# Six copies of the key stack issued from ScalarE's queue instead of SyncE's, in a two-layer attention, mixture and routing kernel

## The chip, the cores and the metric

The kernel runs on one core of one Trainium2 chip. The metric is the device time of one execution in microseconds (us); lower is better. The engines are TensorE (PE: matmuls, and PEld for its weight loads), VectorE (DVE), ScalarE (ACT), GpSimd (POOL) and SyncE (SP). SP does no arithmetic here: it only issues transfers (DMAs). ACT and POOL can issue them too, from queues of their own.

## The reference, cut to what matters

The data are `x`, 8 batches of 256 tokens of width 256, and a context of the same shape. There are four blocks in a row, each added to `x`:

```
x = x + cross_attention, self_attention and gelu FFN   # L0_xattn: two attentions, 16 heads of width 16
x = x + top-2 mixture of 7 experts and a no-op         # L0_ffn
x = x + cross_attention over the same context          # L1_xattn
x = x + gelu FFN on the top half of the tokens         # L1_ffn
# one attention:
q = split_heads(x @ qw + qb); k = split_heads(ctx @ kw + kb); v = split_heads(ctx @ vw + vb)
probs = softmax(q k^T / 4 + mask); out = probs v @ ow + ob
```

## The kernel before, in words

An attention of one batch is an *item*; there are 24 of them, numbered `n`. Items 0 to 7 are the cross attention and 8 to 15 the self attention of the first block; they run as one pipeline in the first third of the kernel. Items 16 to 23 are the third block's attention and form a second pipeline after the experts. Each engine's program is one list, merged by `side_by_side` from small generators: each `yield t` states a planned time in abstract steps, and pieces are put in order of these times. So the order on an engine is fixed, and an instruction that waits for a semaphore holds up everything behind it on that engine. `start_of(n)` is 8 steps after that of the item before; `kv_start(n)` is the same but for item 16.

The arithmetic is fp32 in quality, with each operand split in a high and a low part. For the scores, a head's product over 16 rows is done as one product over 48 rows: the *query stack* `qst` and the *key stack* `kst` hold, for each head pair, three groups of 16 rows (high, high, low against high, low, high), and two more rows for the mask and the row maximum. The stacks are laid out by DMA: `q_parts` and `k_parts` (128 partitions, high and low, two halves `s`) are copied to 16 partitions at a time, six copies for each stack (2 values of `s` by 3 values of `c`), each 128 KB. A stack has three buffers in turn (`NSET`), but `q_parts` and `k_parts` have one each.

One item goes as follows.

- PE transposes the item's rows (L210), projects queries and keys (L186 to L188, `G[0]`). ACT writes the high part of each (`high`, L792) and DVE the low part (`split`, L1163, which raises `q_split` or `k_split`). ACT's `high` of item n first waits until all six copies of item n-1 have landed, since they read the same buffer.
- SP issues the copies (L379). Its list for one item is: two small rows of maxima of an earlier item (L417, which waits for `m_row`), six query copies, for items 0 to 10 two copies of mask rows into `kst` (L396), six key copies (which wait for `k_split`), and then loads from HBM that fall due (raw weights L365, context L372).
- PE waits for both stacks, then runs for each of 8 head pairs `p` the scores (L528, into `S_PS`), from which DVE takes the row maximum (L1207). Later it transposes the maxima (L538); ACT writes them out (`m_hi`, L810, raises `m_row`).
- PE then computes the transposed scores (L549, into `T_PS`) with the maximum's row as part of the product; ACT takes the exponential of each pair (L818). `T_PS` is one buffer: the scores of the next pair wait for the exp before. PE multiplies the probabilities with the values (L588), and ACT copies the result out (L831). Transposes (L562), normalisation, the output projection and LayerNorm follow.

Three items are in work at once: while the scores of item n run, the exps of item n-1 or n-2 and the projections of item n+1 run between them. ACT's list around one item n+1 is: `k_parts` high, `m_hi`, exp, exp, copy out, exp, `hT_hi` (L801), exp, copy out, exp, copy out, exp, `q_parts` high, exp, copy out, `aT_hi` (L824), exp.

Of the kernel before, what the change touches and what calls it, by code (L numbers as in the profile page):

```python
# [6 lines left out]
F32 = mybir.dt.float32  # L7
# [7 lines left out]
B, S, D, H = 8, 256, 256, 16  # L15
DH = D // H
# [3 lines left out]
HG = H // 2  # L20
# [7 lines left out]
MASK_ROW = 3 * DH  # L28
MAX_ROW = MASK_ROW + 2
SROWS = MASK_ROW + 2  # L30
NA = 2 * B
NSET = 3
# [48 lines left out]
def build(nc, x, ctxT, mask, wA, colA, rowA, fi, fo, fib, rw, rb, ein, eout, wC, colC, rowC, w1, w2, b1, out):  # L81
# [14 lines left out]
    with scope[0] as root:  # L96
# [67 lines left out]
        kst, qst = stacks[0::2], stacks[1::2]  # L164
# [62 lines left out]
        ITEMS = range(3 * B)  # L227
# [25 lines left out]
        def kv_start(n):  # L253

            return T_E0 + 5 * E_STEP if n == NA else start_of(n)
# [66 lines left out]
        with nc.Block() as block:  # L322

            @block.sync
            def _(sp):
# [47 lines left out]

                def stack(n, which):
                    j = n % NSET
                    dst = qst[j] if which == "q" else kst[j]
                    for s in range(2):
                        for c in range(3):
                            sp.dma_start(dst[64 * s + DH * c:64 * s + DH * (c + 1), :, :].bitcast(F32), PARTS[which][c][:, s, :].bitcast(F32)).then_inc(sm[f"stk_{which}{j}"], 16)  # L379

                def stack_k(n):
                    j = n % NSET
                    yield kv_start(n) - 6.7
                    if n >= NA + NSET or NSET <= n < NA:
                        sp.wait_ge(sm["st_ps"], HG * (n - NSET + 1))
                    elif n >= NA:
                        sp.wait_ge(sm["kst_one"], n - NA + 1)
                    elif n:
                        sp.wait_ge(sm["init_p"], 2 * n)
                    else:  # L390
                        sp.wait_ge(sm["init_d"], 1)
                    if n < B + NSET:
                        sp.wait_ge(sm["mask_out"], 48)
                        src = mask_dram[n] if n < B else mask_dram[B]
                        for s in range(2):
                            sp.dma_start(kst[j][64 * s + MASK_ROW:64 * s + MASK_ROW + 2, :, :].bitcast(F32), src).then_inc(sm[f"mask_ld{j}"], 16)  # L396
                    sp.wait_ge(sm["k_split"], n + 1)
                    stack(n, "k")

                def stack_q(n):  # L400
# [9 lines left out]
                    else:  # L410
                        sp.wait_ge(sm["init_d"], 1)
                    stack(n, "q")
                    yield t0 + 8.9
# [33 lines left out]
                def store(i):  # L447
# [4 lines left out]
                side_by_side(setup(), weights(), *(context(n) for n in ITEMS if layer(n) != SELF),  # L452
                             *(stack_k(n) for n in ITEMS), *(stack_q(n) for n in ITEMS),
                             *(expert_weights(e) for e in range(NE)), *(expert_tokens(e) for e in range(NE)), *(expert_store(e) for e in range(NE)),
# [311 lines left out]
            def _(act):  # L766
# [14 lines left out]
                def high(n, which, at):  # L781
# [11 lines left out]
                    last.then_inc(sm[f"{which}_hi_s"], 1)  # L793

                def queries(n):
                    t0 = start_of(n)
                    yield t0 - 12.95
                    act.wait_ge(sm["hT_ps"], n + 1)
                    if n:
                        act.wait_ge(sm["v_ps"], n)  # L800
                    act.activation(flat(hT_hi[:]), G[0], ACT.Copy).then_inc(sm["hT_hi_s"], 1)  # L801
                    yield from high(n, "q", t0 - 10.1)
# [88 lines left out]
                def mod(i):  # L891
# [14 lines left out]
                    for m in range(KF):  # L906
                        yield t0 + 1 + 0.4 * m
                        act.wait_ge(sm["mfc1_ps"], 2 * i + m // 4 + 1)
                        if i >= 2 and m == 0:
                            act.wait_ge(sm["mfc2_ps"], i - 1)  # L910
                        act.activation(mg[:, i % 2, m, :], T_PS[:, m * P:(m + 1) * P], ACT.Gelu_apprx_tanh, bias=b1c[:, m:m + 1]).then_inc(sm["mgelu"], 1)

                side_by_side(setup(), *(queries(n) for n in ITEMS), *(high(n, "k", kv_start(n) - 8.1) for n in ITEMS), *(attention(n) for n in ITEMS),
                             *(ffn(f) for f in range(B)), *(route(g) for g in range(len(GROUPS))), *(expert(e) for e in range(NE)),
# [527 lines left out]
```

## Time and profile before

| | |
|---|---|
| median of 3 runs | 1021.02 us (1018.63 to 1021.18) |
| the profiled execution | 1016.88 us, its span 1015.1 us |
| PE busy | 804.1 us, 79% of the span |
| DVE busy | 561.1 us, 55% |
| ACT busy | 425.6 us, 42% |
| DMA queue of SP | 73610 packets, 76.44 MB, 42.1% of the time of 16 DMA engines |
| copies into each of `qst` and `kst` | 144 of 128 KB |

The span is the time from the first to the last instruction; some 2 us of the execution lie around it. A busy share is a mean over stages with different limits, so it tells little of a change in one of them. The first attention pipeline lies between about 45 and 365 us of the span, the experts between 585 and 697, the second attention pipeline between about 745 and 930. In a row of a timeline the first number is the start in us, the second the duration, and the bracket at the end is the idle time of that engine before the instruction and what ended it.

### The profile page before, as it was taken

Reading aid. Unit: us, or ns where it says so; the run is one execution under the profiler, and the core shown is the slowest. Engines: PE = TensorE matmul, PEld = TensorE weight load, DVE = VectorE, ACT = ScalarE, POOL = GpSimd, SP = SyncE. Lnnn points to the kernel's source line nnn. Section 1 sums busy time; section 2 is a strip of 40 time slices with the busy share of each in tenths; the row PEclk is TensorE's granted clock in tenths of the full one; section 3 lists DMA queues with packets and bytes.
Section 4 is the critical chain, followed back from the end, with each engine's and each line's share of the span. In section 5 each row is a group of like instructions: output and inputs, shape, how many; then the busy total and the mean of one; then the engine's idle time right before and its main releaser. Section 6 shows DMA issues by size and latency. Waiting matters only on the chain.

```text
span 1015.1 us, 16969 instructions
## 1 busy us (share of the span) xinstructions
PE 804.1 (79%) x6612; PEld 657.3 (65%) x6612; DVE 561.1 (55%) x1164; ACT 425.6 (42%) x707; POOL 409.2 (40%) x422
## 2 busy tenths in 40 slices
PE   1569999999998878778763299994267989889898
PEld 1456777777776568778763278883155656657897
DVE  4457888888888533444535301212357888864442
ACT  1126666666666664443431011210004656655232
POOL 3744474634434535343374322003883344313200
PEclk9868999999999998887776589997557999989999
DMA  5959777767677022000032154331585676700000
GB/s 193 124 84 177 103 110 109 93 96 99 101 111 100 3 83 105 1 1 1 13 132 89 31 185 170 53 118 57 99 145 74 88 92 86 85 2 2 21 33 32
DMA packets 76940, 83.72 MB, mean 82 GB/s; under 512 B 8863, under 2 KB 72350, under 8 KB 76689
## 3 DMA queue, kind: packets, MB, share of 16 engines
q1 hardware_dynamic: 73610, 76.44, 42.1%
q0 software_dynamic: 3072, 6.04, 2.5%
q8 instruction: 53, 0.87, 0.4%
q14 instruction: 27, 0.21, 0.1%
q10 hardware_dynamic: 178, 0.16, 0.0%
HBM read 36.70 MB, written 10.11 MB: 46 GB/s over the span
## 4 chain that ended last, share of the span: by engine, by line
PE 50%; DVE 13%; DMA 11%; SPq 9%; POOL 8%; issue 6%; ACT 2%; POOLq 0%; DVEq 0%; ACTq 0%
DMA kst<-k_parts 9%; SPq L379 8%; PE ps L186 7%; PE ps L187 6%; PE ps L188 6%; PE ps L528 5%; PE ps L689 5%; DVE nmax L1207 5%; PE ps L703 5%; PE ps L742 3%; PE ps L588 3%; PE ps L549 3%; PE ps L752 2%; POOL gat L1079 2%; POOL moe_in L1067 2%
## 5 line engine op out<-in xcount | busy, mean ns | idle before, releaser
L1207 DVE TENSOR_REDUCE nmax<-ps 128x4 f32<-128x1024 f32 x192 | 235.8, 1228 | 96.9 <-PE ps L528 91.3
L818 ACT ACTIVATE prob<-ps 128x1024 f32<-128x1024 f32 x192 | 196.1, 1021 | 79.6 <-PE ps L549 77.3
L528 PE MATMUL ps<-kst,qst 50*128 50x256 f32 (+1 forms) x768 | 102.5, 347 | 53.3 <-DVE nmax L1207 36.7
L990 POOL TENSOR_TENSOR rstd<-var,half 128x2 f32<-128x2 f32 x56 | 46.5, 830 | 239.8 <-DVE var L1151 182.6
L528 PEld LDWEIGHTS ps<-kst,qst 50*128 50x128 f32 (+1 forms) x768 | 61.3, 197 | 101.8 <-DVE nmax L1207 70.0
L588 PE MATMUL ps<-prob,vext 128*32 128x256 f32 x1536 | 106.2, 395 | 0.6 <-ACT oext L831 0.6
L549 PE MATMUL ps<-qst,kst 51*128 51x256 f32 (+1 forms) x768 | 81.7, 291 | 8.6 <-ACT prob L818 7.9
L1007 POOL TENSOR_TENSOR hres<-hres,rows 128x512 f32<-128x512 f32 x24 | 30.6, 1276 | 114.7 <-PE ps L210 114.7
L210 PE MATMUL ps<-ident,hres 128*128 128x128 f32 x160 | 26.9, 302 | 59.2 <-POOL hres L994 52.3
L549 PEld LDWEIGHTS ps<-qst,kst 51*128 51x128 f32 (+1 forms) x768 | 61.5, 193 | 14.0 <-ACT prob L818 11.4
L1079 POOL DMA_INDIRECT gat<-moe_out,slu x32 | 32.7, 1023 | 79.4 <-DMA moe_out<-vext 70.5
L588 PEld LDWEIGHTS ps<-prob,vext 128*32 128x32 f32 x1536 | 41.1, 111 | 31.9 <-issue 3.3
L994 POOL TENSOR_SCALAR hres<-xres,mv,rstd 128x256 f32<-128x256 f32 x48 | 58.9, 1234 | 2.5
L210 PEld LDWEIGHTS ps<-ident,hres 128*128 128x128 f32 x160 | 20.5, 156 | 60.8 <-issue 53.4
L1342 DVE COPY vext<-ps 128x512 f32<-128x512 f32 x7 | 4.8, 690 | 88.5 <-PE ps L703 54.2
L831 ACT ACTIVATE oext<-ps 128x256 f32<-128x256 f32 x96 | 36.9, 384 | 31.1 <-PE ps L562 25.2
L801 ACT ACTIVATE hT_hi<-ps 128x512 fp32r<-128x512 f32 x24 | 14.3, 598 | 83.8 <-PE ps L210 83.8
L186 PE MATMUL ps<-hT_hi,w_hi 128*128 128x256 f32 x128 | 42.8, 334 | 5.9 <-DVE hT_lo L1154 5.9
L689 PE MATMUL ps<-oext,e_in 128*128 128x256 f32 x160 | 38.8, 403 | 3.4 <-ACT oext L881 3.4
L1067 POOL DMA_INDIRECT moe_in<-hres,slu x32 | 33.5, 1045 | 18.0 <-DVE slu L1333 9.2
L994 POOL TENSOR_SCALAR res<-res,mv,rstd 128x256 f32<-128x256 f32 x32 | 38.9, 1223 | 1.7
L187 PE MATMUL ps<-hT_hi,w_lo 128*128 128x256 f32 x128 | 39.2, 306 | 0.0
(216 smaller groups left out, 2122.4 us busy)
## 6 DMA issues: line engine op xcount, KB each, us to landing
qst<-q_parts SPq DMA_DIRECT2D x144, 128.0 KB, 4.5
kst<-k_parts SPq DMA_DIRECT2D x144, 128.0 KB, 6.3
e_in<-in_ein SPq DMA_DIRECT2D x5, 1024.0 KB, 5.0
e_out<-in_eout SPq DMA_DIRECT2D x5, 1024.0 KB, 8.5
ctx_raw<-in_ctxT SPq DMA_DIRECT2D x16, 256.0 KB
ew_in<-in_ein SPq DMA_DIRECT2D x2, 1024.0 KB, 5.9
ew_out<-in_eout SPq DMA_DIRECT2D x2, 1024.0 KB, 8.7
out<-xres SPq DMA_DIRECT2D x8, 256.0 KB, 2.1
```

The source lines that it names most:

```text
L186: pe.matmul(dst, lhs[0], rhs[0], start=first, stop=False)
L187: pe.matmul(dst, lhs[1], rhs[0], start=False, stop=False)
L188: return pe.matmul(dst, lhs[0], rhs[1], start=False, stop=last)
L379: sp.dma_start(dst[64 * s + DH * c:64 * s + DH * (c + 1), :, :].bitcast(F32), PARTS[which][c][:, s, :].bitcast(F32)).then_inc(sm[f"stk_{wh ...
L528: last = pe.matmul(S_PS[:, 512 * s + S * t:512 * s + S * (t + 1)], qst[j][a:b, p, t * P:(t + 1) * P], kst[j][a:b, p, :], start=True, stop= ...
L549: last = pe.matmul(T_PS[:, 512 * s + S * t:512 * s + S * (t + 1)], kst[j][a:b, p, t * P:(t + 1) * P], qst[j][a:b, p, :], start=True, stop= ...
L588: last = pe.matmul(half_bank[32 * i:32 * i + 32, :], vext[n % NSET][:, t, s * HG + p, :], probs[p % 4][:, s, t, :], start=(t == 0), stop=( ...
L689: last = pe.matmul(pair[:, (m % 4) * S:(m % 4 + 1) * S], win[:, k, m * P:(m + 1) * P], xT[:, k, :], start=(k == 0), stop=(k == KD - 1))
L818: act.activation(probs[p % 4][:].rearrange("p i t s -> p (i t s)"), T_PS, ACT.Exp).then_inc(sm["exp_done"], 1)
L994: last = gp.tensor_scalar(dst[:, t, :], src[:, t, :], mv[i][:, t, 0:1], rstd[i][:, t:t + 1], ALU.subtract, ALU.mult)
L1067: gp.indirect_dma_start(moe_in, bass.IndirectOffsetOnAxis(ap=slu[:, t, r:r + 1], axis=0), hres[:, t, :], None, bounds_check=NE * CAP - 1, ...
L1207: dve.tensor_reduce(nmax[n % 2][:, :, :, p].rearrange("p t s -> p s t"), S_PS.rearrange("p (s t k) -> p s t k", s=2, t=TB), AX.X, ALU.max, ...
```

## The change

The six key copies of an item are issued by ACT, not SP. They stand in ACT's list in three pairs: the first at `kv_start(n) - 6.7` (between the exps of the 7th and the 8th head pair), behind a wait for `k_split` and for the stack buffer to be free; the second at -5.0 (behind the next item's first exp, ahead of `hT_hi`); the third at -4.0 (behind a copy out, ahead of the third exp). The query copies stay on SP, in their place. So do the mask rows, without the wait for `k_split` behind them. No copy, tile, size or wait of PE is changed.

```diff
-                def stack(n, which):
...
-                def stack_k(n):
+                def stack_mask(n):
                     j = n % NSET
                     yield kv_start(n) - 6.7
-                    if n >= NA + NSET or NSET <= n < NA:
+                    if n >= NSET:
                         sp.wait_ge(sm["st_ps"], HG * (n - NSET + 1))
-                    elif n >= NA:
-                        sp.wait_ge(sm["kst_one"], n - NA + 1)
...
-                    sp.wait_ge(sm["k_split"], n + 1)
-                    stack(n, "k")
...
+                def stack_k(n):
+                    j = n % NSET
+                    for i in range(6):
+                        s, c = i // 3, i % 3
+                        if i % 2 == 0:
+                            yield kv_start(n) - (6.7, 5.0, 4.0)[i // 2]
+                        if i == 0:
+                            if n >= NA + NSET or NSET <= n < NA:
+                                act.wait_ge(sm["st_ps"], HG * (n - NSET + 1))
+                            elif n >= NA:
+                                act.wait_ge(sm["kst_one"], n - NA + 1)
+                            elif n:
+                                act.wait_ge(sm["init_p"], 2 * n)
+                            else:
+                                act.wait_ge(sm["init_d"], 1)
+                            act.wait_ge(sm["k_split"], n + 1)
+                        act.dma_start(kst[j][64 * s + DH * c:64 * s + DH * (c + 1), :, :].bitcast(F32), PARTS["k"][c][:, s, :].bitcast(F32)).then_inc(sm[f"stk_k{j}"], 16)
```

The rest of the diff writes the query copies out in `stack_q`, limits the mask generator to items under 11, and adds `stack_k` to ACT's list.

## Rows read from the trace of the kernel before

**Rows 1.** The page's part 4: what the chain that ended last consists of.

```profile
DMA kst<-k_parts 9%; SPq L379 8%; PE ps L186 7%; PE ps L187 6%; PE ps L188 6%; PE ps L528 5%; PE ps L689 5%; DVE nmax L1207 5%; PE ps L703 5%; PE ps L742 3%; PE ps L588 3%; PE ps L549 3%; PE ps L752 2%; POOL gat L1079 2%; POOL moe_in L1067 2%
```

**Rows 2.** All waits: who waited for whom, us in total, times, longest.

```profile
PE ps L528 <- DMA kst<-k_parts: 11.6, 13, 3.6
ACT k_parts L792 <- DMA kst<-k_parts: 16.3, 11, 6.3
```

**Rows 3.** PE's timeline: first scores of items 0, 5, 6, 13, 15, 23.

```profile
43.45 0.50 PE L528 MATMUL ps<-kst,qst 50*128 50x256 f32 x4 [3.63 <-DMA kst<-k_parts]
...
143.80 0.50 PE L528 MATMUL ps<-kst,qst 50*128 50x256 f32 x4 [0.35 <-DMA kst<-k_parts]
...
162.83 0.51 PE L528 MATMUL ps<-kst,qst 50*128 50x256 f32 x4 [0.61 <-DMA kst<-k_parts]
...
293.31 0.50 PE L528 MATMUL ps<-kst,qst 50*128 50x256 f32 x4 [0.20 <-DMA kst<-k_parts]
...
329.28 0.50 PE L528 MATMUL ps<-kst,qst 50*128 50x256 f32 x4 [1.60 <-DMA kst<-k_parts]
...
887.85 0.79 PE L528 MATMUL ps<-kst,qst 48*128 48x256 f32 x4 [2.32 <-DMA kst<-k_parts]
```

**Rows 4.** SP's timeline: groups of six copies, item 6's two among them.

```profile
94.46 5.20 SPq L379 DMA_DIRECT2D kst<-k_parts  x6
...
147.04 3.85 SPq L379 DMA_DIRECT2D qst<-q_parts  x6
...
151.72 3.80 SPq L379 DMA_DIRECT2D kst<-k_parts  x6
...
853.98 5.37 SPq L379 DMA_DIRECT2D qst<-q_parts  x6
```

**Rows 5.** Tile view of `qst`, 144 to 163 us: item 6's six query copies.

```profile
DMA to landing us min/median/max: 3.3/4.4/5.5
```

**Rows 6.** Tile view of `kst`, 651 to 663 us: item 16's key copies alone.

```profile
L379 SPq DMA_DIRECT2D kst<-k_parts x6: 594/606/633, 651.8 to 655.0; - x6
...
DMA to landing us min/median/max: 3.3/4.4/5.3
```

**Rows 7.** DVE's timeline: the low part of item 6's keys.

```profile
145.49 0.87 DVE L1163 SCALAR_TENSOR_TENSOR k_parts<-ps,cols,k_parts 128x256 fp32r<-128x256 f32 x2
```

**Rows 8.** ACT's timeline, 144 to 163 us.

```profile
147.00 1.02 ACT L818 ACTIVATE prob<-ps 128x1024 f32<-128x1024 f32 x1 [0.83 <-PE ps L549]
...
150.88 0.60 ACT L801 ACTIVATE hT_hi<-ps 128x512 fp32r<-128x512 f32 x1 [1.03 <-PE ps L210]
...
153.39 1.02 ACT L818 ACTIVATE prob<-ps 128x1024 f32<-128x1024 f32 x1 [0.42 <-PE ps L549]
...
157.71 0.84 ACT L792 ACTIVATE q_parts<-ps,cols 128x256 fp32r<-128x256 f32 x2 [0.60 <-PE ps L188]
158.43 1.02 ACT L818 ACTIVATE prob<-ps 128x1024 f32<-128x1024 f32 x1
```

**Rows 9.** PE's timeline: transposed scores that follow two of these exps.

```profile
148.39 0.40 PE L549 MATMUL ps<-qst,kst 51*128 51x256 f32 x4
...
160.20 0.40 PE L549 MATMUL ps<-qst,kst 51*128 51x256 f32 x4
```

**Rows 10.** ACT's timeline at the start: a DMA issue and the next activation.

```profile
8.06 0.76 ACTq L779 DMA_DIRECT2D mask_dram<-zeros  x1
8.87 0.63 ACT L773 ACTIVATE w_hi<-prob 128x512 fp32r<-128x512 f32 x1 [4.00 <-issue]
```

**Rows 11.** SP's timeline at the start: two issues of one shape.

```profile
6.89 1.62 SPq L338 DMA_DIRECT2D fibc<-in_fib  x1
...
9.72 0.50 SPq L341 DMA_DIRECT2D b1c<-in_b  x1
```

**Rows 12.** DMA view, 588 to 600 us: GB/s in 40 slices, expert weight loads.

```profile
GB/s 372 355 396 335 335 348 362 352 345 355 270 92 20 24 24 14 0 0 0 0 0 0 0 0 0 0 0 0 0 0 0 0 0 0 0 0 0 0 0 0
```

**Rows 13.** DMA view, 740 to 760 us: the GpSimd queue's packets, MB, share of engines.

```profile
q0 software_dynamic: 503, 1.36, 42.6%
```

More of the change, by code:

```diff
@@ L391, in stack_k @@
                         sp.wait_ge(sm["init_d"], 1)
[L392 to L396, printed above, removed]
-                    sp.wait_ge(sm["k_split"], n + 1)
-                    stack(n, "k")
+                    sp.wait_ge(sm["mask_out"], 48)
+                    src = mask_dram[n] if n < B else mask_dram[B]
+                    for s in range(2):
+                        sp.dma_start(kst[j][64 * s + MASK_ROW:64 * s + MASK_ROW + 2, :, :].bitcast(F32), src).then_inc(sm[f"mask_ld{j}"], 16)
                 def stack_q(n):
@@ L411, in stack_q @@
                         sp.wait_ge(sm["init_d"], 1)
-                    stack(n, "q")
+                    for s in range(2):
+                        for c in range(3):
+                            sp.dma_start(qst[j][64 * s + DH * c:64 * s + DH * (c + 1), :, :].bitcast(F32), PARTS["q"][c][:, s, :].bitcast(F32)).then_inc(sm[f"stk_q{j}"], 16)
                     yield t0 + 8.9
@@ L452, in _ @@
                 side_by_side(setup(), weights(), *(context(n) for n in ITEMS if layer(n) != SELF),
-                             *(stack_k(n) for n in ITEMS), *(stack_q(n) for n in ITEMS),
+                             *(stack_mask(n) for n in ITEMS if n < B + NSET), *(stack_q(n) for n in ITEMS),
                              *(expert_weights(e) for e in range(NE)), *(expert_tokens(e) for e in range(NE)), *(expert_store(e) for e in range(NE)),
@@ L911, in mod @@
                         act.activation(mg[:, i % 2, m, :], T_PS[:, m * P:(m + 1) * P], ACT.Gelu_apprx_tanh, bias=b1c[:, m:m + 1]).then_inc(sm["mgelu"], 1)
-                side_by_side(setup(), *(queries(n) for n in ITEMS), *(high(n, "k", kv_start(n) - 8.1) for n in ITEMS), *(attention(n) for n in ITEMS),
+                side_by_side(setup(), *(queries(n) for n in ITEMS), *(high(n, "k", kv_start(n) - 8.1) for n in ITEMS), *(stack_k(n) for n in ITEMS), *(attention(n) for n in ITEMS),
                              *(ffn(f) for f in range(B)), *(route(g) for g in range(len(GROUPS))), *(expert(e) for e in range(NE)),
```

5 lines of the change are left out of this document (removed).

## The prediction

> **What bounds the kernel now.** I read the page's chain first. Key copies in flight have 9% of it and SP's issuing of copies another 8%, some 170 us together [rows 1]; the reader is to see that this looks like a large prize. The table of waits says how much of it is real: PE stood still for key copies 13 times and 11.6 us in all, ACT 11 times and 16.3 us [rows 2]. The chain follows whatever came last, and here two loops end within half a microsecond of each other, so it names the DMA loop and hides the other one.
>
> The timeline of PE shows both. Items 5 to 13 start 8 periods apart in (293.31 - 143.80) = 149.5 us, so 18.7 us each; the period of item 5 is 19.03 us, of which PE waits 0.61 for keys at its end, which leaves 18.4 us that PE, DVE and ACT need among themselves [rows 3]. Of the 11.6 us, 3.63 are at the first item, 1.60 at item 15 and 2.32 at item 23; the other ten waits share 4.1 us, nearly all in the first pipeline. These are ceilings for what the change can give.
>
> The DMA loop: SP issues item 6's query copies from 147.04 and its key copies from 151.72 to 155.52 [rows 4]; the scores start at 162.83 [rows 3], so twelve copies take 15.75 us. The first query copy lands 3.3 us after its issue, at 150.3, and the last 5.5 us after its own (150.3), at 155.8 [rows 5]: five copies in 5.5 us, 1.1 us each, though they are issued every 0.65. Item 16's six key copies, issued with no query copies around them, go at the same pace (655.1 to 660.3) [rows 6]. So a stack is paced by the moving of data: 6 x 1.1 and 2.2 us of latency, and both 12 x 1.1 + 2.2 = 15.4, close to 15.75. A copy's 128 KB in 1.1 us is 119 GB/s, while expert loads reach 335 to 396 [rows 12]; the DMA engines can do more, but not, one after the other, into 16 partitions each.
>
> **What is removed.** SP loses 3.8 us of issuing for each item. The keys need not stand behind the queries: their low part is ready at 145.49 + 0.87 = 146.36 [rows 7], and SP gets to them at 151.72. SP's HBM loads behind them go out 3.8 us earlier; no wait in my rows hangs on them, so 0. Between the experts SP no longer holds the later loads behind item 16's `k_split`; PE is the bound there, so 0 as well.
>
> **What is added on ACT.** The nearest rows for one issue are SP's 0.60 to 0.61 us plus 0.04 between two [rows 4, 6], and ACT's own 0.76 at the start; the activation behind that one starts when it ends, 4.00 us idle put down to issue [rows 10]. So an issue on ACT takes ACT's time. Lower bound 0 where an exp before it still runs, upper 0.76; I take 0.64, the nearest in shape, 1.28 for a pair and 3.85 for an item, 92 us over 24 items. ACT is 42% busy, so what counts is the place:
>
> - Pair 1 waits for `k_split` at 146.36 and ends near 147.6. The exp at 147.00 had 0.83 us idle before it [rows 8]; it slips 0.65 and ends at 148.65. The next transposed scores, at 148.39 [rows 9], wait for it: PE slips 0.27.
> - Pair 2, behind the next exp, falls into the 1.03 us idle ahead of `hT_hi` at 150.88 [rows 8] and overruns by 0.3, which later gaps take.
> - Pair 3 delays the exp of 153.39 (0.42 idle before it [rows 8]) by some 1 us; the transposed scores that need its end came late enough for that. 0.
>
> So 0.27 us for an item. Bounds: 0 (issue beside running exps, and pair 1 short), 0.5 (0.76 per issue).
>
> An issue can also be slow: 5.20 us for a group of six that mostly takes 3.80 [rows 4]; SP's timeline has 11 such groups (over 4.5 us) among 48, the last at 853.98. For 24 groups on ACT I expect 5 or 6 such stalls of 1.2 us. ACT has no 1.2 us of slack anywhere, so most of it shows: 4 us (bounds 0 and 7).
>
> **What is shared.** Query copies no longer have the DMA engines to themselves. This is the term that decides. The reader should follow `q_parts`: the high part of the next queries overwrites it on ACT at 157.71 and waits for item 6's query copies, landed at 155.8 [rows 5, 8]. That is 1.9 us of margin; behind it the exp at 158.43 ends at 159.45 and PE wants it at 160.20 [rows 9], 0.75 more. Beyond 158.5, each microsecond of late queries is a microsecond of period.
>
> Now keys start at 146.4, queries at 147.04. If two queues take turns at an unchanged pace, all twelve end at 146.4 + 15.4 = 161.8, and the queries, whose last copy is then among the last, land there rather than at 155.8. If they don't disturb each other, 155.8 stays. In rows a second queue is seen only beside GpSimd's gathers: it had 42.6% of the 16 engines' time while SP's queue moved query and key copies [rows 13], so taking turns is real; whether the pace rises when two copies go to different partitions no row shows. I follow the two orders by hand, at half pace where both copy into the same kind of 16 rows (same `s`, and `c` equal or 0 beside 2) and at full pace otherwise: twelve copies then need 9.25 copy times, and the queries land at 146.4 + 9.25 x 1.1 + 2.2 = 158.8. I take this middle. It is 0.3 past the margin. So the period is 18.4 + 0.27 + 0.3 = 19.0 against 18.7: the wait for keys goes, late queries and late exps come.
>
> The Trainium skill, page "DMA: Bandwidth & Descriptors", section "Issuing engines are not separate DMA queues", says that transfers begun on several engines interleave on the same 16 DMA engines and that only the issuing time is saved. Rows 13 agree on the turns. By that rule the pace stays, and the time would be that of the even turns below, not mine.
>
> **The sum**, against the profiled execution (1016.9 us; the median of the runs is 4.1 above it, and I add the change to the median):
>
> - twelve full periods of the first pipeline at +0.3: +3.6
> - its first items, still filling: three at +0.27, less about 1 of the 3.63 us (all data there is in flight already): 0
> - item 15 and item 23: keys earlier by 0.7 to 2: -1.0 and -1.5
> - seven items of the second pipeline at +0.27: +1.9
> - slow issues: +4
>
> Together +7: 1028 us.
>
> **Rivals.**
>
> - *Faster: keys early, queries undisturbed.* The queries stay at 155.8 to 158.5, every wait for keys goes: -4.1 - 1.6 - 2.3 - 2 of the first, and ACT's +0.27 x 20 partly beside running exps, say +2, slow issues +2: -6, 1015 us. It decides if two copies at once move at over 1.25 times the pace of one. For it: 119 against over 335 GB/s [rows 5, 12]. Against: ACT's cost stays.
> - *Even turns at unchanged pace.* Queries land at 161.8, ACT's high part slips 4.1, less 0.75: a period of 18.4 + 0.27 + 3.35 = 22.0, +3.3 for twelve: 40, some 8 in the second pipeline, slow issues 3: 1072 us. It needs both an even share and no gain in pace.
> - *The two issuers block one another.* Pair 1 goes out while SP issues row maxima and queries. If each issue then takes twice as long, the exp of 147.00 slips 1.9, PE 1.6 instead of 0.27: +1.3 for some 19 items, 1021 + 25 + 4 = 1050 us. For it: SP took 1.62 us for one small load during ACT's three issues, 0.50 for its twin later [rows 11]. Against: ACT's own issue was not long then [rows 10]. The Trainium skill, "Perfetto Trace Analysis", section "DMA Instruction — HWDGE (DVE, Sync)", has such a lock: two sequencers share the block that makes descriptors, and an issue's recorded time contains the wait for it.
> - *Nothing.* The keys land as before because the twelve copies take as long, and ACT's issues fit: 1021 us.
>
> **How the numbers follow.** Chances: forecast 0.38, faster rival 0.26, even turns 0.15, blocked issuers 0.12, nothing 0.09. Around the forecast its own terms give +1 to +16 (1022 to 1037). The range reaches from 1012 to 1055: it leaves out most of the even turns and the best end of the faster rival. A measurement here tells about 0.3% (3 us) from no change. Faster takes 0.22 from its rival; within 0.3% takes 0.04 of that one, 0.09 of "nothing" and 0.10 of the forecast; slower is the rest.
>
> **What the profile after would show.** Key copies under ACT's queue at 0.6 us each, in pairs; no wait of L528 for `kst` in the first pipeline; L792 of `q_parts` waiting for DMA `qst` where PE ended its wait before; L818 starting later behind pair 1; slices above 130 GB/s where both stacks move. I am wrong upwards if `q_parts` waits some 4 us per item or ACT's issues are over 1 us; wrong downwards if the query copies still land within 9 us of their first issue and the period is 18.5 or less.

## The result

| | time, us (median, lowest to highest) | ratio to before, 95% interval | span of the profiled run | granted clock |
|---|---|---|---|---|
| before | 1019.83 (1018.50 to 1021.18) | | 1015.1 | 0.888 |
| after | 1041.02 (1036.53 to 1044.28) | 1.0178 [1.014, 1.0216] | 1039.4 | 0.893 |

The change costs 1.8%, by the ratio and its interval (the two medians alone are 21.2 us or 2.1% apart, inside that interval). The forecast was slower by 7 us, 0.7%, in a range from 1012 to 1055 us: the sign is right and the time lies in the range, but the loss is about three times the forecast. Where the time went can be read from the first scores of items 0, 5, 6, 13, 15 and 23 on PE's timeline (before: [rows 3]):

```profile
47.50 0.80 PE L519 MATMUL ps<-kst,qst 50*128 50x256 f32 x4 [2.53 <-DMA kst<-k_parts]
...
153.67 0.51 PE L519 MATMUL ps<-kst,qst 50*128 50x256 f32 x4 [0.56 <-DMA kst<-k_parts]
...
174.09 0.50 PE L519 MATMUL ps<-kst,qst 50*128 50x256 f32 x4 [0.79 <-DMA kst<-k_parts]
...
315.64 0.51 PE L519 MATMUL ps<-kst,qst 50*128 50x256 f32 x4
...
355.38 0.80 PE L519 MATMUL ps<-kst,qst 50*128 50x256 f32 x4 [2.09 <-DMA kst<-k_parts]
...
916.49 0.50 PE L519 MATMUL ps<-kst,qst 48*128 48x256 f32 x4 [1.67 <-DMA kst<-k_parts]
```

Item 0 starts 4.05 us later than before and item 15 26.1 later: eight periods from item 5 to item 13 take 161.97 us where they took 149.5, 20.2 each for 18.7. Item 23 starts 28.6 later, so the second pipeline adds little. The end is 24.3 later: the last stretch takes 122.9 us and took 127.3. Nothing in it was changed. TensorE was granted 0.88 and 0.96 of its full clock in its first two parts before, and 0.96 and 1.00 after; 1.00 is the upper level, 2.4 GHz, and the others are a mix of it with the lower one, 1.2 GHz. PE's busy time in the stretch, 113.5 us and then 109.1, differs by the same 4.4 us. They hide that the order of work lost 28.6 us, not 24.3. They are no merit of the change either: in the runs below the stretch takes 123.2 to 127.3 us, whoever issues the keys. The windows, before and then after (us, busy time of the engines, PEclk, DMA share, GB/s):

```profile
887.90:930.00 42.10, 35.91 (x345) 25.35 (x346) 23.61 (x64) 25.55 (x37) 11.09 (x12) 0.88 0.01 2
930.00:970.00 40.00, 37.40 (x263) 34.29 (x262) 18.11 (x72) 11.16 (x42) 8.89 (x11) 0.96 0.05 15
970.00:1015.10 45.10, 40.18 (x261) 36.04 (x259) 13.77 (x51) 11.63 (x45) 0.80 (x2) 0.99 0.10 34
```

```profile
916.50:958.60 42.10, 35.87 (x375) 24.46 (x375) 25.32 (x72) 25.89 (x37) 13.83 (x15) 0.96 0.01 2
958.60:998.60 40.00, 37.39 (x259) 34.62 (x260) 18.00 (x70) 11.73 (x44) 6.66 (x10) 1.00 0.06 21
998.60:1039.40 40.80, 35.83 (x234) 32.05 (x232) 12.18 (x46) 10.81 (x41) 0.40 (x1) 0.98 0.10 33
```

In the table of waits of after two have grown: the transposed scores (L540) wait 30.0 us for exps, where they waited 7.9, and `q_parts` 21.6 us for its copies, where it waited 2.8. The waits for keys [rows 2] are smaller but not gone, 8.6 us for 11.6 and 11.0 for 16.3:

```profile
PE ps L540 <- ACT prob L827: 30.0, 34, 1.8
ACT k_parts L783 <- PE ps L188: 24.9, 18, 4.9
ACT q_parts L783 <- DMA qst<-q_parts: 21.6, 15, 2.6
ACT k_parts L783 <- DMA kst<-k_parts: 11.0, 5, 6.5
PE ps L519 <- DMA kst<-k_parts: 8.6, 7, 2.5
```

Both grown waits can be seen in one period. ACT's timeline of item 7, to be laid beside [rows 8]; in brackets the idle time before the row and who ended it:

```profile
177.29 1.22 ACTq L802 DMA_DIRECT2D kst<-k_parts  x2
178.60 1.02 ACT L827 ACTIVATE prob<-ps 128x1024 f32<-128x1024 f32 x1 [2.15 <-PE ps L579]
...
180.31 1.03 ACT L827 ACTIVATE prob<-ps 128x1024 f32<-128x1024 f32 x1 [0.41 <-PE ps L540]
180.31 1.36 ACTq L802 DMA_DIRECT2D kst<-k_parts  x2
...
184.08 2.32 ACTq L802 DMA_DIRECT2D kst<-k_parts  x2
186.50 1.02 ACT L827 ACTIVATE prob<-ps 128x1024 f32<-128x1024 f32 x1 [2.04 <-PE ps L579]
...
190.60 0.84 ACT L783 ACTIVATE q_parts<-ps,cols 128x256 fp32r<-128x256 f32 x2 [1.45 <-DMA qst<-q_parts]
```

PE's and SP's timelines at the same place (before: [rows 9] and [rows 4]):

```profile
176.84 0.40 PE L540 MATMUL ps<-qst,kst 51*128 51x256 f32 x4
...
179.77 0.50 PE L540 MATMUL ps<-qst,kst 51*128 51x256 f32 x4 [0.94 <-ACT prob L827]
```

```profile
177.33 4.08 SPq L403 DMA_DIRECT2D qst<-q_parts  x6
181.51 0.81 SPq L387 DMA_DIRECT2D kst<-mask_dram  x2
182.36 0.37 SPq L365 DMA_DIRECT2D wraw<-in_fi  x1
```

Four things are to be seen. The transposed scores of 176.84 end at 177.24; ACT issues pair 1 at 177.29, and only then the exp that needs those scores, 2.15 us idle where it was 0.83: it slips 1.3 us, and PE's next transposed scores stand 0.94. Pair 2 costs nothing, since its issue begins beside a running exp. Pair 3, where one of the two issues was slow (2.32 us for both), holds the exp of 186.50, and PE stands 0.28 us for it at 187.58. And the queries land late: their issue begins at 177.33, and `q_parts`, free of PE long before, is held until 190.60, 13.3 us after that issue. In the tile view, the six query copies of item 7 take

```profile
DMA to landing us min/median/max: 4.5/6.6/9.7
```

where item 6's took 3.3/4.4/5.5 [rows 5]. Over the page's whole table of issues the medians are 6.5 and 8.1 us to landing:

```profile
qst<-q_parts SPq DMA_DIRECT2D x144, 128.0 KB, 6.5
kst<-k_parts ACTq DMA_DIRECT2D x144, 128.0 KB, 8.1
```

### The profile page after: what moved, and what is told of

Its sections match the earlier page's. It is cut to its first block, busy times and chain, and to the rows that moved or that the text cites. A ratio compares the mean times of both kernels' runs of the same rounds, so it can differ in the third digit from the quotient of the medians.

```text
span 1039.4 us, 16980 instructions
## 1 busy us (share of the span) xinstructions
PE 808.1 (78%) x6612; PEld 657.7 (63%) x6612; DVE 562.1 (54%) x1164; ACT 420.5 (40%) x707; POOL 409.4 (39%) x422
## 3 DMA queue, kind: packets, MB, share of 16 engines
q10 hardware_dynamic: 20914, 19.04, 14.1%
## 4 chain that ended last, share of the span: by engine, by line
PE 53%; DMA 13%; DVE 10%; POOL 7%; ACT 6%; issue 6%; ACTq 3%; SPq 2%; POOLq 0%; DVEq 0%
PE ps L186 8%; DMA kst<-k_parts 7%; PE ps L187 7%; PE ps L188 6%; PE ps L680 5%; PE ps L519 5%; PE ps L694 5%; DMA qst<-q_parts 4%; ACT prob L827 4%; PE ps L540 4%; DVE nmax L1216 3%; PE ps L733 3%; PE ps L579 3%; ACTq L802 3%; PE ps L743 2%
## 5 line engine op out<-in xcount | busy, mean ns | idle before, releaser
L827 ACT ACTIVATE prob<-ps 128x1024 f32<-128x1024 f32 x192 | 196.6, 1024 | 114.2 <-PE ps L540 62.7
L519 PE MATMUL ps<-kst,qst 50*128 50x256 f32 (+1 forms) x768 | 101.9, 345 | 47.6 <-DVE nmax L1216 35.3
L519 PEld LDWEIGHTS ps<-kst,qst 50*128 50x128 f32 (+1 forms) x768 | 60.9, 196 | 95.2 <-DVE nmax L1216 68.7
L540 PE MATMUL ps<-qst,kst 51*128 51x256 f32 (+1 forms) x768 | 83.9, 296 | 32.7 <-ACT prob L827 30.0
L579 PE MATMUL ps<-prob,vext 128*32 128x256 f32 x1536 | 103.9, 388 | 0.6 <-ACT oext L840 0.6
L540 PEld LDWEIGHTS ps<-qst,kst 51*128 51x128 f32 (+1 forms) x768 | 60.6, 190 | 44.1 <-issue 21.0
L840 ACT ACTIVATE oext<-ps 128x256 f32<-128x256 f32 x96 | 36.9, 385 | 15.4 <-PE ps L553 10.7
L783 ACT ACTIVATE q_parts<-ps,cols 128x256 fp32r<-128x256 f32 x48 | 20.2, 471 | 54.1 <-PE ps L188 32.5
```

The lines of the kernel that those rows point to most:

```text
L519: last = pe.matmul(S_PS[:, 512 * s + S * t:512 * s + S * (t + 1)], qst[j][a:b, p, t * P:(t + 1) * P], kst[j][a:b, p, :], start=True, stop= ...
L540: last = pe.matmul(T_PS[:, 512 * s + S * t:512 * s + S * (t + 1)], kst[j][a:b, p, t * P:(t + 1) * P], qst[j][a:b, p, :], start=True, stop= ...
L579: last = pe.matmul(half_bank[32 * i:32 * i + 32, :], vext[n % NSET][:, t, s * HG + p, :], probs[p % 4][:, s, t, :], start=(t == 0), stop=( ...
L827: act.activation(probs[p % 4][:].rearrange("p i t s -> p (i t s)"), T_PS, ACT.Exp).then_inc(sm["exp_done"], 1)
```

## The experiments

Each group of runs has its own runs of the kernel before beside it (medians 1022.3 to 1023.4 us, where the result's own had 1019.8), so runs of different groups are compared by their ratios. The table gathers all of them. "Period" is the first scores of item 13 less those of item 3 on PE's timeline, over ten; the last two columns are the median times from the issue of an item's first query copy to the landing of its last query and last key copy, over items 3 to 14.

| kernel | time, us | ratio, 95% interval | period | queries | keys |
|---|---|---|---|---|---|
| before | | | 18.80 | 9.5 | 15.4 |
| after | 1041.02 | 1.0178 [1.014, 1.0216] | 20.43 | 13.1 | 16.4 |
| e1 pair 1 behind exp | 1074.88 | 1.0492 [1.0433, 1.0552] | 21.97 | 13.7 | 16.6 |
| e2 upper half first | 1037.79 | 1.0105 [1.0023, 1.0187] | 20.24 | 12.1 | 16.2 |
| e3 quarter keys | 1028.84 | 1.0041 [1.0004, 1.0078] | 19.54 | 9.5 | 11.7 |
| e4 small issues | 1026.01 | 1.0029 [0.9998, 1.0061] | 19.13 | 8.8 | 15.4 |
| e5 pairs beside exps | 1038.05 | 1.017 [1.0115, 1.0225] | 20.05 | 11.5 | 16.3 |
| e6 pairs after queries | 1028.06 | 1.0071 [1.004, 1.0102] | 19.32 | 9.4 | 15.8 |
| e7 SyncE takes turns | 1084.54 | 1.0596 [1.0529, 1.0663] | 23.17 | 13.8 | 15.2 |
| e8 quarter keys behind exp | 1008.47 | 0.9866 [0.9808, 0.9925] | 18.53 | 10.0 | 11.7 |
| e9 after, loads held | 1041.23 | 1.0192 [1.0146, 1.0238] | 20.02 | 12.4 | 15.4 |
| e10 before, loads held | 1024.16 | 1.0024 [0.9997, 1.0052] | 18.45 | 9.6 | 14.9 |
| e11 e6, loads held | 1023.23 | 1.0003 [0.997, 1.0035] | 18.69 | 9.6 | 15.0 |
| e12 before, held from item 3 | 1016.31 | 0.9959 [0.9926, 0.9992] | 18.48 | 9.4 | 14.9 |
| e13 after, held from item 3 | 1037.08 | 1.0126 [1.0076, 1.0176] | 20.06 | 12.5 | 15.5 |
| e14 e6, held from item 3 | 1022.93 | 0.9996 [0.9965, 1.0027] | 18.70 | 9.3 | 15.0 |
| e15 item 0 after hT | 1043.14 | 1.0195 [1.0128, 1.0262] | 20.35 | 12.8 | 16.6 |

**Place or sharing?** Two theories at first: pair 1 stands between scores and their exp (place), or the keys hold up the queries (sharing). Here pair 1 goes behind the exp that it held up.

```diff
-                            yield kv_start(n) - (6.7, 5.0, 4.0)[i // 2]
+                            yield kv_start(n) - (6.35, 5.0, 4.0)[i // 2]
```

> The first pair of key copies stands behind the exp of the 8th head pair, not ahead of it; all else as in the changed kernel. Place theory (in the changed kernel the pair waits for the transposed scores of the buffer's last user, which are the very scores that the next exp waits for, so its 1.2 us of issue lie whole between scores and exp, and PE slips 1.0 us per item): the period of the first pipeline falls from 20.4 to about 19.5 us, the wait of L540 for L827 from 30 us to under 10, and the time to some 1029 us. Sharing theory (the query copies land 12 to 13 us after their first issue, as they take turns with the key copies, and hold up q_parts): the pair goes out 1.3 us later, queries land at the same place or 0.5 us earlier, the time stays at 1038 to 1041 us.

Slower by another 34 us: both expectations missed. ACT's timeline shows the hold gone, as the place theory says, and what came instead:

```profile
136.69 1.02 ACT L827 ACTIVATE prob<-ps 128x1024 f32<-128x1024 f32 x1 [0.82 <-PE ps L540]
136.75 1.21 ACTq L802 DMA_DIRECT2D kst<-k_parts  x2
...
138.52 1.31 ACTq L802 DMA_DIRECT2D kst<-k_parts  x2
...
150.94 0.84 ACT L783 ACTIVATE q_parts<-ps,cols 128x256 fp32r<-128x256 f32 x2 [4.02 <-DMA qst<-q_parts]
```

Pair 2 now follows pair 1 by 1.8 us instead of 3.0. The queries of this item, issued from 136.73, land 14.1 us after their first issue, 0.9 later than the 13.2 of item 7 in after (medians: 13.7 and 13.1), and all that ACT had gained waits for them: 1.45 + 1.3 + 0.9 makes 3.65 of the 4.02 us. PE then stands for longer, and its clock, 1.00 in the change, falls to a mix of the two levels, which lengthens the rest: 194 matmuls are busy for 20.71 us in the first of these windows, where 191 had taken 18.50 in after (174 to 194 us, clock 1.00):

```profile
219.00:242.00 23.00, 20.71 (x194) 15.89 (x194) 15.56 (x26) 12.41 (x19) 7.65 (x7) 0.87 0.62 72
242.00:266.00 24.00, 20.35 (x199) 15.37 (x200) 15.56 (x26) 12.48 (x20) 8.18 (x14) 0.93 0.61 69
```

**Do other partitions help?** The keys in the other order of halves, so that a key copy and the query copy beside it go to different partitions:

```diff
-                        s, c = i // 3, i % 3
+                        s, c = 1 - i // 3, i % 3
```

> Key copies with s = 1 go first, then s = 0, so that keys and queries in flight together go to different halves of the partitions. Theory that the pace is set by the partitions written: two copies at once move faster than one, queries land 9 to 10 us after their first issue instead of 12 to 13, slices of the DMA view rise over 160 GB/s where both move, the wait of q_parts for qst (21.6 us) goes, the time is 1028 to 1033 us. Theory that 16 DMA engines have one pace for such copies whatever the place: nothing changes, 1041 us. Place theory alone: 1041 us as well.

The queries land at 12.1 instead of 13.1, the keys at 16.2 instead of 16.4, the period falls by 0.2 us. The time, 1027 to 1042 us in four runs, can't be told from the change's. All twelve together are hardly quicker, where the forecast's overlap would have had all of them down some 12 us after the first issue, so the assumption that copies into different rows overlap is wrong.

**A quarter of the bytes.** This kernel copies 64 of 256 columns of the keys, and its output is not the attention's; the issues are as many and in the same places.

```diff
-                        act.dma_start(kst[j][64 * s + DH * c:64 * s + DH * (c + 1), :, :].bitcast(F32), PARTS["k"][c][:, s, :].bitcast(F32)).then_inc(sm[f"stk_k{j}"], 16)
+                        act.dma_start(kst[j][64 * s + DH * c:64 * s + DH * (c + 1), :, 0:64].bitcast(F32), PARTS["k"][c][:, s, 0:64].bitcast(F32)).then_inc(sm[f"stk_k{j}"], 16)
```

> Each key copy moves 64 of 256 columns, so its output is not the attention's; the number of issues, their places and waits are those of the changed kernel. Sharing theory: queries land within 10 us of their first issue, q_parts no longer waits for them, nor L519 for keys, the period falls to 19.4 us (18.4 and the slip of pair 1), the time to 1025 to 1029 us. Place theory: the slip of 1 us per item stays, so at least 1036 us if it is all of the loss.

**Issues alone.** The kernel before, with six 8 KB copies for each item (from a constant to a spare buffer) issued on ScalarE at the places of the change, behind the same two waits:

```diff
+                        act.dma_start(junk[16 * (6 * n + i):16 * (6 * n + i + 1), :], ident[0:16, :]).then_inc(sm["junk"], 16)
```

> The kernel before, all stack copies on SP, and on ACT six issues per item of 8 KB each (128 columns of 16 rows to HBM) at the places and behind the waits of the changed kernel's key copies. They cost ACT about as much to issue and move next to nothing. Place theory: PE slips 1.0 us per item, 22 items, 1035 to 1042 us. Sharing theory: under 1024 us. If both hold: the period is near 19.4 us, 1031 to 1036 us, and it and the run with quarter keys agree.

e3 has the queries back at 9.5 and a period of 19.54, as the sharing theory said; the time, 1028.8 us, fits it too. e4 has a period of 19.13 and 1026.0 us, less than the 1031 to 1036 expected if both theories hold, and the two runs don't agree as they were to. The rows at pair 1 in e3 and then in e4:

```profile
149.93 1.22 ACTq L802 DMA_DIRECT2D kst<-k_parts  x2
151.25 1.02 ACT L827 ACTIVATE prob<-ps 128x1024 f32<-128x1024 f32 x1 [2.14 <-PE ps L579]
```

```profile
128.58 0.78 ACTq L805 DMA_DIRECT2D junk<-ident  x2
129.46 1.02 ACT L830 ACTIVATE prob<-ps 128x1024 f32<-128x1024 f32 x1 [1.70 <-PE ps L551]
```

The exp's idle time is 0.83 us in [rows 8], 1.70 with a pair of 0.78 and 2.14 with a pair of 1.22: the slip is the issue's length plus 0.1. The pair of 8 KB copies is issued in 0.39 us each (0.44 in the median of 144), the pair of 128 KB in 0.61, which is the likely reason why e4 costs less than e3. So the issues cost 0.74 us of a period's 1.63 when the keys are short (19.54 less 18.80), and full-size keys the other 0.9 (20.43 less 19.54).

**The cross-check.** Two kernels that each have only one of the causes. First, no issue on ScalarE at all: the kernel before, with SyncE issuing two copies of the queries, two of the keys, and so on, behind a wait for `k_split` (item 16 apart).

```diff
-                    sp.wait_ge(sm["k_split"], n + 1)
-                    stack(n, "k")
...
-                    stack(n, "q")
...
+                        sp.wait_ge(sm["k_split"], n + 1)
+                        for i in (0, 2, 4):
+                            for which, dst in (("q", qst[j]), ("k", kst[j])):
+                                for s, c in ((i // 3, i % 3), ((i + 1) // 3, (i + 1) % 3)):
+                                    sp.dma_start(dst[64 * s + DH * c:64 * s + DH * (c + 1), :, :].bitcast(F32), PARTS[which][c][:, s, :].bitcast(F32)).then_inc(sm[f"stk_{which}{j}"], 16)
```

> The kernel before, with all twelve copies still issued by SyncE, but in turns: two of the queries, two of the keys, and so on (item 16 apart, whose keys come long before). Nothing is on ScalarE. Sharing theory: the last query copy is the tenth of twelve, 10 x 1.09 + 2.2 = 13.1 us after the first issue where it was 9.2; q_parts, ready 10.7 us after that issue, waits up to 2.4 us; period 20.4 to 21.2, time 1040 to 1055, slower than before without one issue on ScalarE. If the loss of the change is that of ScalarE's issues alone: 1021, no change.

Then e3 with pair 1 where e1 has it (a quarter of the key columns again):

> The key copies carry 64 of 256 columns (the keys in three quarters of the stack are stale, the output is not the attention's), and pair 1 stands behind the exp that it held up, as in the first experiment. Theory now (pair 1's place costs 1.3 us of hold, the loss of the first experiment was the queries' later landing and the clock that fell with it): with the sharing nearly gone the hold is gone too, period 19.54 - 0.8 = 18.5 to 18.8 with clock 1.0, time 1010 to 1018, under the kernel before. Rival (moving pair 1 behind the exp makes the engines' order worse in itself, whatever the copies' size): as slow against its twin as the first experiment was, 1029 + 30 = about 1060.

e7 is the slowest of all, 1084.5, with ACT not touched: its queries land at 13.8, `q_parts` waits 88.8 us in the whole run where it waited 2.8, and PE's clock is 0.84 to 0.95 in the stretches of its periods. That is sharing without any issue on ScalarE, and larger than the 1040 to 1055 us expected. Not all of it is sharing: 12.7 us are lost by item 3 already, where the first items' query copies now wait for `k_split` too (item 0's begin at 33.50 us for 27.45). In the periods that follow this wait doesn't bind: in one of them `k_parts` is written at 166.97 and the copies begin at 171.50. e8 is the fastest of all, 1008.5 (1010 to 1018 expected): with little to share, the move that cost e1 34 us gains 20 over e3. Both signs as the theory has them; that the order of engines in e1 is bad in itself is out.

```profile
ACT q_parts L800 <- DMA qst<-q_parts: 88.8, 19, 12.0
PE ps L557 <- ACT prob L826: 45.4, 22, 3.5
```

**Moving the pairs back.** All three pairs beside running exps, first early (e5), then behind the queries (e6):

```diff
-                            yield kv_start(n) - (6.7, 5.0, 4.0)[i // 2]
+                            yield kv_start(n) - (5.3, 4.3, 3.35)[i // 2]
...
-                            yield kv_start(n) - (6.7, 5.0, 4.0)[i // 2]
+                            yield kv_start(n) - (4.3, 3.35, 2.35)[i // 2]
```

> The three pairs each go directly behind an exp (2 to 7 us after the first query copy is issued, where the change has 0, 3 and 6.7), so that they are issued beside it. Sharing theory (the key copies that are issued beside the query copies hold the queries up, and q_parts of the next item waits for that): the queries land 11 to 12 us after their first issue instead of 13.3, the wait of q_parts for them (1.5 us an item) is mostly gone, the keys still land at 16 to 17: period 19.0 to 19.4, time 1022 to 1028. Place theory (only the hold of 1.3 us by pair 1 counts): 20.4 - 1.3 = 19.1 too, but with the queries' landing unchanged at 13.3. A third one, that any issue on ScalarE costs its length on the chain wherever it stands: 1041 as the change.

> The pairs one exp later still, 4.6 to 9 us after the first query copy, about where SyncE issued the keys in the kernel before (4.9 to 8.7). Sharing theory: queries land at 9 to 10 us as before, keys at 15.5 to 16.5, so that only the wait of k_parts of the next item can grow by 0.5 us: period 18.7 to 19.2, time 1019 to 1026. Place theory: as the one before this. If the change of queue itself (two queues in place of one) slows the copies, the keys land later than 16.5 and the time is above 1030.

e5 was to give 1022 to 1028 us and gave 1038. The waits of PE for exps fell to 14.6 us in all (30.0 in the change), but `q_parts` still waits 21.9 us for queries, and `k_parts` 22.5 for keys (11.0 in the change). Of the queries of items 3 to 14, eight land at 10.9 to 11.7 and one at 12.2; in the three items whose six query issues took over 5 us instead of 4 they land at 12.9 to 13.6, since their late copies fall behind the keys: `q_parts` waits 2.78 us in one item, 1.01 in the next, and `k_parts` 1.84 for the keys. So a slow issue of SyncE seems to cost more when a second queue fills the gap than where all stood in one queue [rows 4]; no run separates that.

```profile
186.17 0.84 ACT L783 ACTIVATE q_parts<-ps,cols 128x256 fp32r<-128x256 f32 x2 [2.78 <-DMA qst<-q_parts]
...
204.41 0.84 ACT L783 ACTIVATE q_parts<-ps,cols 128x256 fp32r<-128x256 f32 x2 [1.01 <-DMA qst<-q_parts]
...
209.79 0.84 ACT L783 ACTIVATE k_parts<-ps,cols 128x256 fp32r<-128x256 f32 x2 [1.84 <-DMA kst<-k_parts]
```

e6 has the queries undisturbed at 9.4 and gets back the larger part: +0.7% of the +1.8% are left, 1028 us for the 1019 to 1026 expected. With as many issues on ScalarE as e5, it also excludes the theory that an issue costs its length wherever it stands. Of what is left, 5.9 us are there at item 3 already (111.18 for 105.30), and the periods, 19.32 for 18.80, have the keys landing at 15.8 for 15.4.

**SyncE's loads.** In the change nothing holds SyncE's 256 KB loads behind the key copies: the chunk of weights goes out 5.0 us after the first query copy (182.36 less 177.33, above), where the kernel before had it at 8.5. These three hold such loads until the key stack ahead of them has landed:

```diff
+                        m = int((T_CHUNK[i] - 8 + 6.7) // STEP)
+                        if i < 12 and 0 <= m < NA:
+                            sp.wait_ge(sm[f"stk_k{m % NSET}"], 96 * used(m))
...
+                    if 2 <= n < NA:
+                        sp.wait_ge(sm[f"stk_k{(n - 2) % NSET}"], 96 * used(n - 2))
```

> The change, and SyncE holds its 256 KB loads (the context of item 2 on, a chunk of weights) until the key stack has landed that stood ahead of them on its queue in the kernel before. In the change nothing stands ahead of them, and they go out 3 to 3.5 us earlier, among both stacks' copies. Theory that this sharing counts: the first scores of item 0 come at 44 to 45 us instead of 47.5, the keys land 0.5 to 1 us earlier in items with a load, about 20 loads in the first pipeline: time 1033 to 1038. Rival (the loads cost nothing where they stand; the start slipped because the copies hold ScalarE's hT_hi of the next item): item 0 still at 47, time 1041.

> The kernel before with the same hold of the loads. Its k_parts waits 1.0 to 1.2 us for the key stack of the item before where 0.6 is the floor that the runs with quarter keys showed; if the loads behind the key copies cause a part of it: 1 to 5 us less, 1015 to 1019. If the copies' own pace causes all of it, no change, 1020; if something now waits for a load that comes too late, above 1023.

> The pairs at the places of the experiment that put them behind the queries (1028), with the loads held as well: SyncE's order of transfers in the kernel before, but the six copies issued by ScalarE beside its exps. If issuer and place cost nothing there, 1018 to 1024, the same as before within 0.3%; if 1028 stays, the rest is that the last copy of a pair sequence comes 1 to 1.5 us later than SyncE's.

The periods fall in all three, by 0.35 to 0.63 us, but the time falls only in e11 (1.0003 for e6's 1.0071). From item 2 to item 3 they take 25.2, 25.3 and 26.2 us, where the kernels without the hold took 21.5, 18.6 and 19.3. SyncE's timeline of e10 shows why: the context load at 83.75 waits for item 2's keys, the fourteen zero stores stand behind it, and item 2's maxima row (92.22, before 88.23) behind these.

```profile
83.75 0.41 SPq L377 DMA_DIRECT2D ctx_raw<-in_ctxT  x1
84.21 7.09 SPq L345 DMA_DIRECT2D moe_in<-zeros  x14
...
92.22 1.43 SPq L422 DMA_DIRECT2D qst<-m_hi  x2
```

The same with the hold from item 3's keys on (`3 <= m < NA` and `5 <= n < NA`), and one on the start, item 0's pairs at 4.9, 4.85 and 4.8, behind `hT_hi` of item 1:

> The kernel before, its loads held until the key stack ahead of them has landed, but only from item 3's keys on, so that the zero stores behind one early load aren't put off. If the hold's periods (18.4 where the kernel before has 18.8) are the loads' doing, item 15 starts 3 to 5 us earlier: 1015 to 1018. Rival (the 1024 of the run that held all loads was no slip of the zero stores): above 1022.

> The change with the same hold. Period 20.0 as in the run that held all loads (20.4 without), item 3 no longer 5 us late: 1034 to 1038. Rival: the hold does nothing in the change, since the queries' landing (13 us after their first issue) sets the period and no load lies in it: 1041.

> ScalarE issues the keys behind the queries, loads held from item 3's keys on. Period 18.6 to 18.7, without the 5 us at item 3: 1016 to 1021, faster than the change by 2% and the same as or up to 0.4% faster than the kernel before. If the issues on ScalarE cost something there that the loads hid: 1023 to 1028.

> The change, with item 0's six copies placed behind ScalarE's hT_hi of item 1, which stands behind four of them in the change and ends 3.2 us later than in the kernel before. If that is the start's loss: item 1's q_parts back at 36.5 to 37.5 us (40.2 in the change), its first scores 2 to 4 us earlier, time 1037 to 1039. If the loss is the keys' late landing (47.46 against 43.41): first scores of item 0 still at 47.5 or later, time 1041 to 1043.

e12 is faster than both kernels: 1016.31, 0.41% less than before [0.08% to 0.74%], by waits on SyncE alone. That is the time expected (1015 to 1018), though item 15 starts only 2.1 us earlier and not 3 to 5. Its period is 18.48, its `k_parts` waits 8.0 us in all for keys (16.3 in [rows 2]):

```profile
ACT k_parts L797 <- DMA kst<-k_parts: 8.0, 4, 5.8
```

In the change the hold from item 3 on (e13) takes the period from 20.43 to 20.06; in time it may give some 4 us, as expected, but the intervals overlap ([1.0076, 1.0176] and [1.014, 1.0216]), and e9 shows no gain. With the pairs behind the queries and the loads held (e14, e11) the time is that of the kernel before, between the two outcomes foreseen for e14. Against its twin with SyncE as issuer, e12, e14 is 6.6 us slower by the medians and 0.2 by the period; the intervals of the two overlap, so whether the issuer in itself costs up to 0.6% or nothing is not settled. e15 did not move the time: `q_parts` of item 1 came at 38.33 (36.33 before, 40.24 after), item 0's scores at 46.1. So there is no sign that the time hangs on ScalarE's order at the start.

## Why the prediction was off

**The terms that held.** An issue on ScalarE was taken at 0.64 us; it is 0.617 in the median of 144. Pair 2 costs nothing, as said. The second pipeline took +1.1 us (item 16 to 23) for the +1.9 forecast, but not for the reason given: a period there lasted 20.5 us before (143.82 us for seven), about what the change made of the first pipeline's, so the longer loop adds little. Two of the signs came: `q_parts` waits for `qst`, and L827 starts late behind pair 1. The two signs of an error upwards did not: `q_parts` waits 1.4 us on average, not 4, and the issues are not over 1 us.

**Terms that came out otherwise, with little weight.** Slow issues: 10 of 144 over 0.9 us, the longest 2.00, where 5 or 6 of 1.2 us were expected. Their price, +4, shows at most in part: from item 6 to item 14 the five periods with such an issue take 20.37 us on average, the four without one 20.14. Items 15 and 23 were to gain 1.0 and 1.5 us by earlier keys; their waits went from 1.60 to 2.09 and from 2.32 to 1.67, so they gained -0.5 and 0.65. The waits of L519 for keys fell from 13 to 7 but did not go. The forecast had slices above 130 GB/s where both stacks move; the DMA view of after, 177 to 195 us in 40 slices, has most of them between 100 and 146, and so has that of before, 144 to 163 us:

```profile
GB/s 5 18 0 109 305 146 107 112 102 137 107 109 105 107 137 107 162 109 102 141 114 139 118 125 130 146 100 89 134 196 216 175 125 130 41 23 21 0 0 0
```

**The first step that failed: "Pair 1 waits for `k_split` at 146.36 and ends near 147.6."** The code in front of pair 1 has two waits. The other, for `st_ps` of the item three before (its last transposed scores free the buffer), ends last: SyncE's query copies, which have the same wait, start at 147.04 [rows 4], and the transposed scores end when the exp of 147.00 starts [rows 8]. The row for it was at hand. So pair 1 can't begin before the very event that the exp waits for, and its whole issue falls between the two: the exp slips 1.3 us and not 0.65, PE stands 0.94 at that point and not 0.27. This is the term that was mis-sized most: 0.27 us of a period in the forecast, 0.7 (e3 less before) to 1.0 us (e3 less e8, where only the hold differs) in the runs; the first is less since the short keys also end the wait of `k_parts`.

**The second: the queries "land at 146.4 + 9.25 x 1.1 + 2.2 = 158.8", or 11.8 us after their first issue.** The 9.25 took copies into different rows to overlap. They don't: e2 gains 0.2 us in twelve copies. Twelve copies take 16.4 us in the change and took 15.4 before; with the loads out of the way it is 15.4 to 15.5 (e9, e13) against 14.9 (e10, e12). The prediction's own 12 x 1.1 + 2.2 = 15.4 for no overlap is near all of them, and two queues are not quicker than one but slower by 0.5 to 1.0 us. With no gain in pace the queries come at 13.1 (medians), 1.3 later than the forecast and 3.5 later than before. `q_parts`, itself later by the hold, waits 1.45 us for them where it idled 0.60 before [rows 8]: 0.85 us more of idle time on ScalarE in that period, where 0.3 was put down. Even turns, the rival with unchanged pace, had them at 161.8, 14.8 after the first issue. They landed 1.7 us earlier than that; the likely reason is that pair 3 comes 6.8 us after pair 1, when most query copies are through. In e1 and e7, where the keys follow more closely, the queries land at 13.7 and 13.8 and the times are 1075 and 1085, near the rival's 1072, with a fallen clock that the rival did not have in its sum. So the rival had the right mechanism, and the forecast lay between it and no sharing. The other three are out: SyncE's six query issues beside pair 1 took 4.08 us for 3.85 [rows 4], no doubling; the faster rival needed the queries to land within 11.5 us; and "nothing" is excluded by the interval. The rule of the Trainium skill that the prediction cites (page "DMA: Bandwidth & Descriptors", section "Issuing engines are not separate DMA queues": transfers of several issuers interleave, and only issuing time is saved) is borne out: the twelve copies interleave, and no time of theirs is saved (16.4 us for 15.4; with the loads held 15.4 to 15.5 for 14.9).

**The third, small: "no wait in my rows hangs on them, so 0"** for SyncE's loads that go out earlier. Nothing waits for them, but they move in the same engines: 0.4 us of a period in the change (20.43 less 20.06, e13; 20.02 in e9) and 0.3 in the kernel before (18.80 less 18.48, e12), where the time falls by 0.41%. In the change the medians of e13 say 3.9 us, within the scatter. It is priced by what they slow, not by who waits for them.

**The fourth: "its first items, still filling", at 0.** Item 0's scores came 4.05 us later and item 3's 6.1. Item 0's key copies stand in front of `hT_hi` of item 1 on ScalarE (36.17 for 32.95), and its keys land at 47.46 for 43.41. From the first query copy to the landing of the last key this is 18.9 us for 16.0 before; it is 18.1 to 19.6 in the changed kernels with full-size keys that don't hold the loads at the start (e1, e2, e5, e6, e13, e14, e15), and 15.4 in e9 and e11, which do. So the loads make these 3 us (in e9 the scores then start 1.2 us after the landing, at 44.9). The other 1.1 is that item 0's first query copy was itself issued later (28.52 for 27.45); the runs have it anywhere from 26.6 to 29.0 (e7 apart), in no order that goes with the edits.

In the sum: 12 x 0.3 = 3.6 became about 12 x 1.6 = 20 in round figures (105.3 to 329.28, 223.98 us, before; 111.36 to 355.38, 244.02 us, after), the start and the first items 6.1, the stretch between the pipelines 1.5, the second pipeline 1.1, and the clock in the last stretch gave 4.4 back: 24.3 together. Of a period's 1.6, the experiments give 0.7 to 1.0 to the place of the issues, 0.4 to the loads (20.43 less 20.02 or 20.06), and what remains, 0.2 to 0.5, to the keys among the queries. The shares depend on the order in which the causes are taken away: without the hold (e1) the keys cost far more, since ScalarE then reaches `q_parts` earlier and waits longer, and the clock falls.

## What to carry to other kernels

Before you move an issue ahead of an instruction, ask of every wait in front of it which ends last: if it is the event that the instruction itself waits for, the whole issue lands on the path; behind the instruction it may cost nothing. A second queue for copies that are paced by moving data doesn't make them faster, it only decides whose copies are late; keep the stack that is needed first ahead of the other, and put transfers that nobody waits for behind both (0.4% here). A transfer that nothing waits for still has a price.

## What the runs showed of the hardware

- Copies of 128 KB between partitions, in packets of 1 KB, went at about 1.1 us each. Twelve took 14.9 to 15.4 us from one queue and 15.4 to 16.4 from two that interleaved, and the order of halves (e2) changed that by 0.2. With both stacks in flight the DMA engines showed 0.9 busy at 100 to 146 GB/s.
- ScalarE issues a copy beside an activation that already runs (180.31 and 180.31 above), but the next activation starts only when the issue is over (the pair of 177.29 ends at 178.51, the exp starts at 178.60).
- An issue's length differed with the copy: 0.39 us for 8 KB from 16 partitions, 0.61 us for 128 KB from 128.
- TensorE's granted clock fell to a mix of both levels, 1.2 and 2.4 GHz, in e7 (0.84 to 0.95 of full speed, period by period) and in some periods of e1 (down to 0.87), where `q_parts` waits for queries 4.7 us on average in e7 (88.8 us in 19 waits) and 3.6 in e1 (57.3 in 16), and PE behind it; in the change, with 1.4 (21.6 in 15), the periods of items 4 to 10 stayed at 1.00. The clock is then a price on top of the wait: 20.71 us for 194 matmuls at 0.87, 18.50 for 191 at 1.00.
